# First pair's queries directly behind the latents, and eight of the first sixteen maxima inside the first two attention blocks

## The reference, cut to what matters

```python
q = (x @ Wq.T).reshape(b, t, N_HEADS, HEAD_DIM)        # 8 heads of 64
kv_latent = x @ Wkv_down.T                             # 64 wide
k = (kv_latent @ Wk_up.T).reshape(b, t, N_HEADS, HEAD_DIM)
v = (kv_latent @ Wv_up.T).reshape(b, t, N_HEADS, HEAD_DIM)
scores = jnp.einsum('bqhd,bkhd->bhqk', q, k) * HEAD_DIM ** (-0.5)
attn = jax.nn.softmax(scores, axis=-1)
out = jnp.einsum('bhqk,bkhd->bqhd', attn, v).reshape(b, t, N_HEADS * HEAD_DIM)
return out @ Wo.T

x = x + 0.5 * _L0_ffn_ref(_layernorm(x, axis=-1), ...)
x = x + _L0_attn_ref(_layernorm(x, axis=-1), ...)
x = x + 0.5 * _L0_ffn_ref(_layernorm(x, axis=-1), ...)
```

## Time and profile before

| | |
|---|---|
| median of 3 runs | 1072.6 us (1072.52 to 1073.0) |
| the profiled execution | 1074.65 us |
| its span | 1072.8 us |
| TensorE busy | 960.4 us, 90% of the span |
| VectorE busy | 700.3 us, 65% |
| GpSimd busy | 686.5 us, 64% |
| ScalarE busy | 475.4 us, 44% |
| TensorE's mean granted clock | 0.952 |
| first of the 16 first maxima, on VectorE | at 173.34 us |
| attention blocks of pair 0, batch 0, on TensorE | from 194.47 to 236.13 us |

### The profile page before, as it was taken

How to read it: one execution, slowest core, us unless ns; L and a number is a source line. 1 busy time by engine, 2 the same in 40 slices (tenths; PEclk the granted TensorE clock), 3 DMA queues, 4 the chain that set the end, 5 groups by cost and what they waited for, 6 DMA issues and landing times.

```text
span 1072.8 us, 14511 instructions
## 1 busy us (share of the span) xinstructions
PE 960.4 (90%) x5024; PEld 515.9 (48%) x5024; DVE 700.3 (65%) x1139; ACT 475.4 (44%) x765; POOL 686.5 (64%) x392
## 2 busy tenths in 40 slices
PE   6279966997999989999999999999999999896995
PEld 4168732443444454444445544444454444355884
DVE  4845468566778674776776566777666668676663
ACT  4824431443434435444543454444324444634663
POOL 0055350486989916677774577678637778885775
PEclk9679957798999999999999999999999999998998
DMA  9435421026011010000001000000100030005441
GB/s 328 157 108 160 131 74 69 6 78 176 11 15 16 11 69 1 1 1 1 1 1 69 1 1 1 1 1 1 69 2 1 1 118 1 1 34 189 138 140 48
DMA packets 39733, 59.92 MB, mean 56 GB/s; under 512 B 5866, under 2 KB 33518, under 8 KB 38640
## 3 DMA queue, kind: packets, MB, share of 16 engines
q1 hardware_dynamic: 17664, 25.14, 7.0%
q0 software_dynamic: 8736, 17.91, 6.1%
q10 hardware_dynamic: 13264, 15.97, 4.4%
HBM read 27.50 MB, written 25.85 MB: 50 GB/s over the span
## 4 chain that ended last, share of the span: by engine, by line
PE 64%; DVE 19%; POOL 7%; ACT 3%; issue 3%; DMA 2%; ACTq 1%; POOLq 0%; SPq 0%; DVEq 0%
PE ps_o L1290 15%; PE ps L1277 10%; DVE maxes L1113 8%; PE ps L1107 8%; PE ps L843 7%; DVE rows_store L1664 5%; PE ps_x L1087 5%; POOL arena_b L1766 4%; PE ps L1439 3%; PE ps_x L1312 3%; PE ps L827 2%; PE ps_o L859 2%; PE ps_x L859 1%; ACT rows_store L761 1%; DMA x_res<-x_in 1%
## 5 line engine op out<-in xcount | busy, mean ns | idle before, releaser
L1113 DVE TENSOR_REDUCE maxes<-ps 128x2 f32<-128x1024 f32 x256 | 310.7, 1217 | 196.9 <-PE ps L1107 196.3
L1766 POOL TENSOR_TENSOR arena_b<-arena_b 128x1024 f32<-128x1024 f32 x112 | 272.3, 2437 | 178.6 <-PE ps_o L1290 142.7
L1766 POOL TENSOR_TENSOR arena_b<-arena_b,hot_store 128x1024 f32<-128x1024 f32 x108 | 262.8, 2433 | 68.2 <-PE ps_o L1290 35.0
L1277 PE MATMUL ps<-q_split,keys_now 64*128 64x512 f32 x1536 | 205.3, 392 | 0.0
L1523 ACT ACTIVATE arena_b<-ps 128x1024 f32<-128x1024 f32 x144 | 143.3, 1023 | 101.6 <-PE ps L1277 101.6
L1277 PEld LDWEIGHTS ps<-q_split,keys_now 64*128 64x128 f32 x1536 | 145.3, 186 | 32.9 <-issue 4.1
L1290 PE MATMUL ps_o<-arena_b,latent_now 128*64 128x512 f32 x576 | 148.2, 616 | 1.3 <-ACT arena_b L1523 1.3
L1523 ACT ACTIVATE hot_store<-ps 128x1024 f32<-128x1024 f32 x112 | 112.0, 1022 | 57.5 <-PE ps L1277 57.5
L1290 PE MATMUL ps_o<-hot_store,latent_now 128*64 128x512 f32 x448 | 116.0, 614 | 2.5 <-ACT hot_store L1523 2.5
L1664 DVE RECIPROCAL rows_store<-rows_store 128x256 f32<-128x256 f32 (+1 forms) x72 | 112.6, 1564 | 6.5 <-ACT rows_store L1534 6.5
L1107 PE MATMUL ps<-keys_max_now,q_split 64*128 64x512 f32 x384 | 94.1, 486 | 7.6 <-DVE maxes L1113 6.4
(11 more groups left out here) (325 smaller groups left out, 1138.3 us busy)
## 6 DMA issues: line engine op xcount, KB each, us to landing
sorted_y<-arena_b ACTq DMA_DIRECT2D x40, 128.0 KB, 2.0
x_res<-sorted_x SPq DMA_DIRECT2D x32, 130.0 KB, 2.4
x_res<-x_in SPq DMA_DIRECT2D x4, 1024.0 KB, 13.8
scaled_x<-rows_store SPq DMA_DIRECT2D x16, 256.0 KB, 2.1
keys_now<-keys_next SPq DMA_DIRECT2D x4, 1024.0 KB, 4.5
sorted_x<-blank ACTq DMA_DIRECT2D x2, 1560.0 KB, 13.0
sorted_x<-blank ACTq DMA_DIRECT2D x2, 1430.0 KB, 10.2
arena_a<-w_gu SPq DMA_DIRECT2D x1, 2048.0 KB, 14.3
```

The source lines that it names most:

```text
L1113: nc.vector.tensor_reduce(maxes[:, 2 * m:2 * m + 2], bank[:, :, :], AX_X, ALU.max) \
L1277: last = nc.tensor.matmul(ps_s[n % 2][:, a, :], keys_now[h, key, k], query[h, p, q], start=False, stop=(kt >= KT - STRIDE and query is q_h ...
L1766: nc.gpsimd.tensor_tensor(t, t, prob(k, kt).rearrange("p a n -> p (a n)"), ALU.add) \
```

## The change

Five edits, all for batch 0 and pair 0:

- TensorE makes pair 0's two query groups directly behind the latents, ahead of turning the latents back. Pair 1's two groups come between the maxima, ahead of pieces 2 and 4. The groups' banks are 0, 1, 6 and 0 (`FIRST_QUERIES`).
- VectorE takes tiles 12 to 15 and the variance ahead of the keys, then the keys, the remainders of pair 0's queries and the latent rows.
- Eight of the 16 first pieces (`FIRST_MAXES`) are made ahead of the attention, alternating between `ps[1]` and `ps[2]`; the first shift is transposed right behind them.
- The other eight are made in blocks 0 and 1 of pair 0 (`EXTRA_BLOCKS`), four a block, in `ps[2]`; the second shift's reduction moves from block 0 to block 2.
- Pair 1's 16 pieces are made in pair 0's blocks 2 to 7 instead of 0 to 7, as 3, 3, 2, 3, 3 and 2. Inside a block a piece now stands between the two value steps where four are left, ahead of the first scores and between the two scores where two or more are left, and the rest behind the scores. With two a block that is the order of before.

```diff
@@ -81,7 +81,9 @@
 EARLY = RING * EARLY_GROUPS
 JOINED = NT // 2
 MAX_PIECES = MAXES // BLOCKS
-BACK = QT + ROW_PAIRS + 2
+FIRST_MAXES = MAXES // 2
+FIRST_QUERIES = (0, 1, 6, 0)
+EXTRA_BLOCKS = 2
 TILES = {"f1": SLOT_TILES, "f2": SLOT_TILES_2}
 DONE = {"f1": 0, "f2": SLOT_TILES}
 TURN = {"a": 1, "b": 2}
@@ -1217,6 +1219,20 @@
         SUM_B = PAIRS * 2 * (KT - 1) - 1
         NORM_B = PAIRS * 2 - 1 + QUARTERS
 
+        def max_pieces(first_batch, last_batch, p, d):
+
+            if last_batch and p == PAIRS - 1:
+                return []
+            if first_batch and p == 0 and FIRST_MAXES < MAXES:
+                left = MAXES - FIRST_MAXES
+                if d < EXTRA_BLOCKS:
+                    return [(0, FIRST_MAXES + m) for m in range(left)[d * left // EXTRA_BLOCKS:
+                                                                      (d + 1) * left // EXTRA_BLOCKS]]
+                blocks = BLOCKS - EXTRA_BLOCKS
+                at = [-(-n * MAXES // blocks) for n in range(blocks + 1)]
+                return [(1, m) for m in range(at[d - EXTRA_BLOCKS], at[d - EXTRA_BLOCKS + 1])]
+            return [(p + 1, m) for m in range(d * MAX_PIECES, (d + 1) * MAX_PIECES)]
+
         def pe_attention(pe):
 
             for i in range(ROW_PAIRS):
@@ -1224,17 +1240,26 @@
             pe.wait_ge(sem("columns_ready"), ROW_PAIRS)
             for j in range(2):
                 pe_latents(pe, 0, j, banks[4 + j])
+            for n in range(2):
+                pe_queries(pe, 0, n, n * HALF, banks[FIRST_QUERIES[n]])
             for j in range(2):
                 pe_turn_latents(pe, 0, j, banks[4 + j])
-
-            for n in range(4):
-                pe_queries(pe, n // 2, n % 2, (n % 2) * HALF, banks[n])
-            pe.wait_ge(sem("q_lo"), 2)
-            pe.wait_ge(sem("lat_rows"), 2)
-            for m in range(MAXES):
-                pe_max(pe, 0, m, keys_max_next, max(m - 1, 0), ps[2 - 2 * (m % 2)])
+            pe.wait_ge(sem("q_hi"), 2)
+            pe.wait_ge(sem("lat_hi"), 2)
+            for m in range(FIRST_MAXES):
+                if m == 1:
+                    pe.wait_ge(sem("lat_rows"), 2)
+                if m == 2:
+                    pe_queries(pe, 1, 0, 0, banks[FIRST_QUERIES[2]])
+                if m == 4:
+                    pe.wait_ge(sem("q_lo"), 2)
+                    pe_queries(pe, 1, 1, HALF, banks[FIRST_QUERIES[3]])
                 if m == MAXES // 2:
                     pe_shift(pe, 0, 0)
+                pe_max(pe, 0, m, keys_max_next, max(m - 1, 0), ps[1 + m % 2])
+            if FIRST_MAXES == MAXES // 2:
+                pe_shift(pe, 0, 0)
+            pe.wait_ge(sem("max_taken"), FIRST_MAXES)
             pe.wait_ge(sem("q_lo"), 4)
             pe.wait_ge(sem("batch_ready"), 48)
             pe.wait_ge(sem("q_fill"), 4)
@@ -1405,26 +1430,30 @@
 
                 for p in range(PAIRS):
                     for d in range(BLOCKS):
-                        todo = list(range(d * MAX_PIECES, (d + 1) * MAX_PIECES)) if max_next(p) else []
-
-                        def piece():
-                            if todo:
-                                m = todo.pop(0)
-                                if m == 0:
-                                    pe.wait_ge(sem("q_lo"), 2 * PAIRS * b + 2 * (p + 1) + 2)
-                                pe_max(pe, (p + 1) % PAIRS, m, keys_max_next if p == PAIRS - 1 else keys_max_now,
-                                       MAXES * PAIRS * b + MAXES * (p + 1) + m, ps[2])
+                        todo = max_pieces(first_batch, last_batch, p, d)
+
+                        def piece(count):
+                            if len(todo) >= count:
+                                q, m = todo.pop(0)
+                                if m == 0 and q:
+                                    pe.wait_ge(sem("q_lo"), 2 * PAIRS * b + 2 * q + 2)
+                                pe_max(pe, q % PAIRS, m, keys_max_next if q == PAIRS else keys_max_now,
+                                       MAXES * PAIRS * b + MAXES * q + m, ps[2])
                         before_values(p, d)
                         if p == 0 and d == 0:
                             pe.wait_ge(sem("batch_ready"), 48 * b + 48)
                         if p or d:
                             for s in (2 * d - 2, 2 * d - 1):
                                 values(p - (d == 0), s % STEPS)
+                                if s == 2 * d - 2:
+                                    piece(4)
                         after_values(p, d)
-                        piece()
+                        piece(2)
                         scores(p, 2 * d)
+                        piece(2)
                         scores(p, 2 * d + 1)
-                        piece()
+                        while todo:
+                            piece(1)
                 for s in (STEPS - 2, STEPS - 1):
                     values(PAIRS - 1, s)
 
@@ -1479,8 +1508,9 @@
             for j in range(2):
                 act_latents(act, 0, j, banks[4 + j])
             for n in range(4):
-                act_queries(act, n // 2, n % 2, n, banks[n])
-            act_std(act, "att", QT, JOINED, 1)
+                act_queries(act, n // 2, n % 2, n, banks[FIRST_QUERIES[n]])
+                if n == 1:
+                    act_std(act, "att", QT, JOINED, 1)
             act_shift(act, 0, 0)
             act.wait_ge(sem("row_scale_att"), 2)
 
@@ -1615,25 +1645,24 @@
             for i in range(ROW_PAIRS):
                 dve_norm_rows(dve, 0, i)
                 gathered(QT + i)
+            for t in range(QT + ROW_PAIRS, JOINED):
+                gathered(t)
+            dve_variance(dve, "att", QT, JOINED)
             for j in range(2):
                 dve_keys(dve, 0, j, banks[4 + j])
-                gathered(QT + ROW_PAIRS + j)
+
+            def queries(n):
+                dve_queries(dve, n // 2, n % 2, n, banks[FIRST_QUERIES[n]])
+            queries(0)
+            queries(1)
             for j in range(2):
                 dve_latent_rows(dve, 0, j, banks[4 + j])
-
-            def queries(n):
-                dve_queries(dve, n // 2, n % 2, n, banks[n])
-            for t in range(BACK, JOINED):
-                gathered(t)
-            queries(0)
-            queries(1)
-            dve_variance(dve, "att", QT, JOINED)
-            for m in range(MAXES):
-                dve_max(dve, m, m, ps[2 - 2 * (m % 2)])
+            for m in range(FIRST_MAXES):
+                dve_max(dve, m, m, ps[1 + m % 2])
                 if m == 1:
                     dve_scale(dve, "att", QT, JOINED, 1)
-                if m in (3, 6):
-                    queries(m // 3 + 1)
+                if m in (3, 5):
+                    queries(2 + (m - 3) // 2)
                 if m == MAXES // 2 - 1:
                     dve_shift(dve, MAXES // 2, 0, 0)
 
@@ -1684,14 +1713,16 @@
                 for p in range(PAIRS):
                     g = PAIRS * b + p
                     for d in range(BLOCKS):
-                        todo = list(range(d * MAX_PIECES, (d + 1) * MAX_PIECES)) if max_next(p) else []
+                        todo = max_pieces(first_batch, last_batch, p, d)
+                        half = (len(todo) + 1) // 2
 
                         def pieces(n):
-                            for m in todo[:n]:
-                                dve_max(dve, m, MAXES * PAIRS * b + MAXES * (p + 1) + m, ps[2])
+                            for q, m in todo[:n]:
+                                dve_max(dve, m, MAXES * PAIRS * b + MAXES * q + m, ps[2])
                             del todo[:n]
-
-                        if d == 0:
+                        late_shift = first_batch and p == 0 and FIRST_MAXES < MAXES
+
+                        if d == (EXTRA_BLOCKS if late_shift else 0):
                             dve_shift(dve, MAXES * (g + 1), 2 * g + 1, 1)
                         if d == 5 and max_next(p):
                             dve_shift(dve, MAXES * (g + 1) + MAXES // 2, 2 * g + 2, 0)
@@ -1716,13 +1747,13 @@
                                 dve_slots_late(dve, "a", 0, AHEAD)
                             elif d == 6:
                                 dve_codes_early(dve, small[:, 5, :])
-                        pieces(1)
+                        pieces(half)
                         if not last_batch and p in (1, 2) and d == 0:
                             dve_keys(dve, b + 1, p - 1, ps_x[:, :])
                         if d in QUERY_BLOCKS and queries_next(p):
                             c = QUERY_BLOCKS.index(d)
                             dve_queries(dve, (p + 2) % PAIRS, c, 2 * PAIRS * b + 2 * (p + 2) + c, ps_x[:, :])
-                        pieces(1)
+                        pieces(half)
 
                 def add_projected(t):
                     dve.wait_ge(sem("projected"), QT * b + t + 1)
```

## The result

The changed kernel takes 1074.94 us (median of 9 runs, 1072.72 to 1076.28) against 1072.41 us before (9 runs, 1071.34 to 1073.0): ratio 1.0022, interval 1.0013 to 1.0031, so 2.4 us slower where 0.9 us faster was forecast. Its profiled execution took 1073.65 us, a span of 1071.8, which is 1.0 us *less* than the span of before; the two profiles alone would have confirmed the forecast. Which of the two to believe is the first thing to settle.

What follows compares the result with a forecast made beforehand. TensorE bounds the kernel except in stages; VectorE bounds the first maxima ahead of the attention. Terms -14.4 + 6.5 + 7.0 = -0.9 us take the median from 1072.6 to 1071.7; range 1068.7 to 1075.9.

Steps and rivals of the forecast that it cites:

- rival E: Blocks with three maxima: TensorE's clock falls to half, 2.25 us a fall; 1073.9 with one, 1076.2 with two; 0.05 from two.
- part 4: Blocks 2 to 7: 1.75 us more in each of four blocks with three maxima, 7.0 us back.
- part 3: Blocks 0 and 1: late maxima on the single bank and the shift's wait take 16.3 against 9.82, 6.5 us back.
- Part 1: Ahead of the attention: reordering lets VectorE start the first maximum at 165.45 instead of 173.34, 7.9 us earlier.
- Part 2: Ahead of the attention: eight maxima fewer, the shift's way left without cover; blocks start 14.4 us earlier in all.
- Rival A: Pair 0's blocks: late maxima cost only TensorE's 3.4 us; 9.0 us faster, 1063.6; chance 0.07.
- B: Ahead of the attention and block 0: clock returns a block earlier or is never lost; 1.7 us more gain, 1070.0; 0.17.
- C: Block 1: clock stays at half through it, 3.9 us more; 3.0 slower, 1075.6; chance 0.09.
- D: Ahead of the attention: first maximum less early, a gather or copy being late; slower from 3 us (1074.7); chance 0.04.

Runs made afterwards that it cites:

- filled_wait: Changed kernel plus two idle matmuls (512 and 256 columns) in TensorE's wait for the second shift; 1072.16 us, 0.9995 of before.
- order_clean: Kernel before with only the new order ahead of the attention, all 16 first maxima there, first shift transposed behind the ninth; 1064.89 us, 0.9931 of before.
- changed_filled: filled_wait plus idle matmuls behind maxima 4 to 7, around the first shift's transposition and ahead of block 0's last maximum; 1069.64 us, 0.9984 of before.
- twelve_clean: order_clean with twelve first maxima ahead of the attention instead of 16, so four late ones; 1069.38 us, 0.9971 of before.
- halves: Changed kernel with each maximum in pair 0's blocks split by head, one bank written while the other is reduced; 1070.16 us, 0.9979 of before.
- late_only: Changed kernel with before's order ahead of the attention put back, keeping only the late maxima; 1081.82 us, 1.0093 of before.
- before_filled: Kernel before plus an idle matmul of 256 columns behind each of maxima 4 to 15; 1078.08 us, 1.0058 of before.
- order_filled: order_clean plus an idle matmul of 256 columns behind each of maxima 4 to 15; 1060.62 us, 0.9891 of before.
- shift_in_3: Changed kernel with the second shift's transposition moved from the head of block 2 to the head of block 3; 1070.80 us, 0.9988 of before.

## Why the prediction was wrong

**The direction fell with one step.** The prediction weighed a clock that "falls to half inside the blocks with three maxima" as its rival E, gave it 0.05 from two falls on and took one fall (1073.9) as a case inside its range, with the argument that TensorE would be busy for some 80% of such a block. The step that failed is that part 4 takes block 2 at the full clock, behind three waits that part 3 had laid out itself: their length is in the sum, their effect on the clock is in it at nothing. In the runs the clock fell in the last of these waits, and block 2 took 9.33 and 8.36 us where those terms give 6.73; two idle matmuls in that wait brought 6.73 us back and 2.9 by the medians (filled_wait). With them the change is -0.5 us (-1.5 to +0.4), and the forecast was -0.9. The measured 1074.94 lies 1.0 above the price of one fall.

E as it was worded isn't what came either. Blocks 3, 5 and 6 of the changed kernel each have two waits of 0.62 to 0.86 us, and the clock stays at 1.00 through them; where a profile shows it lost inside the blocks, it was behind a wait of 1.12 to 1.62 us, for block 0's last maximum or for the shift. The Trainium skill (TensorE: Matmul & The Clock Gate, A second HAM failure mode: psum-queue depth-cycling) was cited beside E: TensorE idles so often between groups of matmuls that its clock goes to and fro. The traces agree in part: behind such waits TensorE ran for some 3 to 7 us at 0.50 and came back to 1.00, but the frequent waits of blocks 3, 5 and 6 left it at 1.00.

Point by point:

- **Part 1, the first maximum 7.9 us earlier: right.** From the latents' start to the first reduction it was 173.34 - 153.93 = 19.4 us before and is 161.36 - 150.80 = 10.6, so 8.8 less; 0.5 of it are the latents' matmuls (5.18 us instead of 5.68), whose clock came back earlier in this execution. order_clean gives -7.4 (-8.7 to -6.0) for the part alone.
- **Part 2, the cover lost: right.** From the end of the shift's reduction to the blocks' first maximum 176.02 - 173.14 = 2.9 us, as laid out. The DMA's landing never held the scores here; in changed_filled, where all else was quicker, it did by 0.39 us.
- **Part 3, 6.5 us back in blocks 0 and 1: right**, 16.39 against 9.82.
- **Part 4, 1.75 us in each block with three maxima: right, but for the clock.** Block 3 took 7.85 against 7.9; blocks 2 to 7 took 38.90 us in filled_wait and in twelve_clean, 7.06 more than before, and 41.49 in the changed kernel. Block 2 is the one that was 2.6 over.
- **The cause of those waits, one double bank: shown** by halves, whose block 3 has 0.26 us of idle TensorE instead of 1.26. The block is only 0.5 us shorter for it; the median is 4.7 us lower.
- **Rival A** (late maxima cost only 3.4 us of matmuls) is refuted by late_only and by the 7.06 us. **B** didn't happen: the clock was lost among the maxima, and is 0.81 over blocks 0 and 1. **C** didn't: block 1 ran at the full clock up to the wait for the shift. **D** didn't: the first maximum was early.
- **The range.** It ends at 1075.9; the prediction says that A alone lies beyond it, but E with two falls, 1076.2, does too.
- **The sum against one profile.** It was made on the profile of before whose stretch was 82.2 us; the second has 81.6. That is no error of the change's price but a reason to distrust a margin of 0.9.

Left open: why the same wait loses the clock in one execution and not in another, and how often each kernel's clock falls where. Each profile shows one case, and a run's mean clock only hints at it: of the changed kernel's twenty runs the two with the highest, 0.958 and 0.957, are the fastest of their batches (1072.72 and 1072.85 us), and even they aren't below before's medians.

## What to carry to other kernels

Price a wait on TensorE twice, once for its length and once for the clock: here the waits of 0.63, 0.63 and 1.62 us cost 1.6 to 2.9 us more than they lasted, and idle matmuls in the longest of them gave that back. Moving work from an engine-bound stretch to one where that engine has room pays only if the buffer it goes through has room as well; here two scores filled the bank's cycle exactly, and each further maximum cost 1.75 us for 0.43 us of matmuls. And when a change has two halves, time them apart: the order alone was worth 7.4 us (11.7 with fillers) and the other half, at 10.0, gave it all back.

## What was not expected of the hardware

- Idle matmuls keep a clock but needn't win it back: TensorE with an instruction for 23.00 of 23.00 us stayed at 0.50 (before_filled), while with fillers of the same size, begun at 1.00 and with TensorE busy for 13.26 of 15.00 us, it held (order_filled). The Trainium skill (TensorE: Matmul & The Clock Gate, What's actually happening) says that activity releases the throttle; in these 23 us, busy by their records, it stayed. Which property of the fillers matters was not tried.
- The length of a wait doesn't tell whether the clock is lost. A wait of 1.62 us for the second shift lost it in three profiles (changed twice, late_only) and one of 1.12 us in halves, but 1.62 us did not in twelve_clean's. A wait of 1.32 us ahead of block 0's last maximum lost it in two profiles (shift_in_3, late_only) and not in three (changed twice, filled_wait).
- Two reductions of 512 columns take 1.29 us where one of 1024 takes 1.22, so splitting a maximum over two banks costs VectorE 6%. The two, in halves:

```profile
178.81 1.29 DVE L1127 TENSOR_REDUCE maxes<-ps 128x1 f32<-128x512 f32 x2 [3.71 <-PE ps L1120]
```
